# Layer 0's cross-attention: Pool's side jobs thinned out, queries loaded by pairs of groups, one transfer of shift rows a group

## The chip, the core and the metric

The kernel runs on one core of a Trainium2 chip. Its time is that of one execution on the device, in microseconds. The core has TensorE (PE: matmuls; PEld: its weight loads), VectorE (DVE), ScalarE (ACT), GpSimd (POOL) and SyncE (SP), which here only issues DMAs. Each engine has its own instruction stream, and they wait for each other by semaphores. TensorE's granted clock has two levels, 1.2 and 2.4 GHz.

## What is computed

Two transformer layers on x of 8 samples, 512 tokens and 320 features, with a context of 64 tokens and 192 features a sample. Each layer has self-attention, cross-attention to the context and a gated feed-forward, each behind a layer norm and with a residual. Layer 1 has also quantization to 8 bits in its attentions. The part in question, of layer 0:

```python
def _attn(x, ctx, wq, wk, wv, wo, bo, heads):       # heads = 20, dh = 16
    q = (x @ wq).reshape(b, n, heads, dh).transpose(0, 2, 1, 3)
    k = (ctx @ wk).reshape(b, j, heads, dh).transpose(0, 2, 1, 3)
    v = (ctx @ wv).reshape(b, j, heads, dh).transpose(0, 2, 1, 3)
    a = softmax(einsum('bhid,bhjd->bhij', q, k) * dh ** -0.5, axis=-1)
    return einsum('bhij,bhjd->bhid', a, v).transpose(0, 2, 1, 3).reshape(b, n, heads * dh) @ wo + bo
...
h2 = _ln(x, n2_g, n2_b)
x = _attn(h2, context, q2, k2, v2, o2_w, o2_b, heads) + x
h3 = _ln(x, n3_g, n3_b)
a, g = split(h3 @ ff_w1 + ff_b1, 2)
x = a * gelu(g) @ ff_w2 + ff_b2 + x
```

## The kernel before

`transformer` calls one function a phase, each with a block of its own that all engines enter and leave together. For layer 0: `dense_phase` (q, k, v), `self_attention`, `dense_phase` ("q": output projection of the self-attention, queries of the cross-attention), `cross_attention`, `dense_phase` ("ff"). Products in float32 precision are made of parts: each weight is held as `hi` and `lo` (`Split`), and each activation as well.

`cross_attention` (1892 to 2184) works in 40 groups of 4 heads of one sample (`NQ` = 40, `PER` = 5 groups a sample). In a group, two heads stand together in each of two halves `pr`. A group passes through these steps:

- SP loads the queries into `q_stack`, a ring of 8 groups (`RING`), three DMAs a group (hi, hi, lo; L1976), keys of a sample (six DMAs, L1966) and values (two, L1986).
- TensorE's `natural`: 8 matmuls of scores with the tokens on the partitions (`nat`, L2030). DVE takes the negated maximum of each row, `neg_max` (L2169).
- Pool splits `neg_max` into three bf16 parts with four instructions (`parts`, L2129 to L2132). The tile `parts` is single: Pool waits until TensorE has turned those of the group before.
- TensorE turns the parts into rows (`turn_shift`, L2047), ACT copies them to `shift_sb` (L2102) and issues two DMAs from it into rows 96 to 101 of `q_stack`, one a half (L2105).
- TensorE's `transposed`: the scores once more with keys on the partitions, the maximum taken off by those rows (`sT`, L2039). ACT makes the exponentials, `probs` (L2097).
- TensorE's `products` with the values (`o_ps`, L2057), ACT's copy `o_sb` (L2111), TensorE's `turn_output` (L2065), DVE's division and `o_nat`, SP's store to `cross_out` (L2013).

The order is written out by hand: all engines count n from -3 to 42, and TensorE does in round n `natural(n + 3)`, `transposed(n)`, `turn_shift(n + 2)`, `turn_output(n - 2)`, `products(n - 1)`. ACT does in round n the exponentials of n, the shift rows of n + 2 and the copy of `o_sb` for n - 1.

Pool has side work behind the `parts` of each group n. `PoolLoader.turn(pool, n)` (L274) starts the transfer of weight job n into one of two stage buffers and splits job n - 1 into `hi` and `lo` (L261 to L271); there are ten jobs, two for `wo2`, two for the first 256 rows of `ff_w2` and six for its other 1024 rows. `EarlyBias.add` (L306) adds the output bias to a 128-token tile of the residual x, 32 tiles in all, in groups 0 to 31.

`dense_phase` "ff" starts with the output projection of the first sample, statistics, `rstd` on Pool (L808), the norm, the transposes `zT` and then `ff1` and `ff2` products over ten chunks (`ff2` at L895). Where it is called with `next_weights`, as in layer 1, Pool runs all jobs of its loader directly behind the first `rstd`, before its bias add of the first sample (L824), and TensorE waits for them before the first chunk that is not in `ws[1]`.

Of the kernel before, what the change touches and what calls it, by code (L numbers as in the profile page):

```python
# [25 lines left out]
ALU = mybir.AluOpType  # L26
# [4 lines left out]
P = 128  # L31
# [3 lines left out]
FF = 1280  # L35
# [61 lines left out]
def words(t):  # L97

    return t.bitcast(F32)


def rows(ap, start, n):
    return ap[bass.ds(start, n), :]
# [1793 lines left out]
def cross_attention(nc, s, k, q, kk, v, out, next_weights, bias):  # L1897
# [3 lines left out]
    ROWS = QROWS + 6  # L1901
    N_Q, N_K, N_V = 3, 6, 2

    with ExitStack() as ctx:
# [21 lines left out]
        def exists(n):  # L1926
            return 0 <= n < NQ
# [12 lines left out]
        def shift_bank(n):  # L1940
# [6 lines left out]
            **{f"x_q_loaded{r}": 16 * N_Q * NQ // RING for r in range(RING)},  # L1947
            **{f"x_k_loaded{r}": 16 * N_K * len(range(r, BATCH, KEYS)) for r in range(KEYS)},
            **{f"x_v_loaded{r}": 16 * N_V * BATCH // 2 for r in range(2)},
            **{f"x_shift_loaded{r}": 32 * NQ // 2 for r in range(2)},  # L1950
# [19 lines left out]
        with nc.Block() as block:  # L1970

            @block.sync
            def _(sp):
                def load_q(n):
                    for quadrant, part in enumerate((0, 0, 1)):
                        sp.dma_start(words(q_stack[32 * quadrant:32 * quadrant + 32, n % RING]),  # L1976
                                     rows(q[part], n * 64, 64).rearrange("(x r) t -> r x t", r=32)
                                     ).then_inc(s[f"x_q_loaded{n % RING}"], 16)
# [13 lines left out]
                for n in range(1, LOOK):  # L1992
                    load_q(n)
                wait(sp, "x_cleared", 2)
                load_v(0)
                for n in range(LOOK, RING):
                    load_q(n)
# [3 lines left out]
                for n in range(FIRST, LAST):  # L2001
                    b = n // PER
                    if exists(n - 1) and exists(n - 1 + RING):
                        wait(sp, "x_turn_free", uses["scores", n - 1] + 1)
                        load_q(n - 1 + RING)
                    if exists(n - 1) and n % PER == 0 and b - 1 + KEYS < BATCH:
                        load_k(b - 1 + KEYS)
# [12 lines left out]
            def _(pe):  # L2020
                def natural(n):
                    wait(pe, f"x_q_loaded{n % RING}", 16 * N_Q * (n // RING + 1))
# [12 lines left out]
                def transposed(n):  # L2035
                    wait(pe, f"x_shift_loaded{n % 2}", 32 * (n // 2 + 1))
# [46 lines left out]
            def _(act):  # L2083
# [9 lines left out]
                for n in range(FIRST, LAST):  # L2093
# [5 lines left out]
                    if exists(n + 2):  # L2099
                        wait(act, "x_turn_full", uses["shift", n + 2] + 1)  # L2100
                        wait(act, f"x_shift_loaded{n % 2}", 32 * ((n + 2) // 2))
                        act.copy(shift_sb[:, n % 2, :], shift_bank(n + 2)).then_inc(s["x_turn_free"], 1)  # L2102
                        wait(act, "x_turn_free", uses["shift", n + 2] + 1)
                        for pr in range(2):
                            act.dma_start(words(q_stack[QROWS:ROWS, (n + 2) % RING, pr, :]),  # L2105
                                          words(shift_sb[6 * pr:6 * pr + 6, n % 2, :])
                                          ).then_inc(s[f"x_shift_loaded{n % 2}"], 16)
# [6 lines left out]
            def _(pool):  # L2114
# [9 lines left out]
                for n in range(NQ):  # L2124
                    wait(pool, "x_nat_free", 2 * (n + 1))
                    wait(pool, "x_turn_full", uses["shift", n - 1] + 1 if n else 0)
                    mine = neg_max[:, n % 4]
                    one, two, three = (parts[:, :, i:12:3] for i in range(3))
                    chained(pool.tensor_copy(one, mine), 3 * n + 1)  # L2129
                    chained(pool.tensor_tensor(rest[:, :, :], mine, one, ALU.subtract), 3 * n + 2)  # L2130
                    chained(pool.tensor_copy(two, rest[:, :, :]), 3 * n + 3)
                    pool.tensor_tensor(three, rest[:, :, :], two, ALU.subtract).then_inc(s["x_parts_ready"], 1)  # L2132
                    wait(pool, "x_parts_ready", n + 1)
                    loader.turn(pool, n)
                    if n < BATCH * TT:
                        early.add(pool, n)

            @block.vector
            def _(dve):
# [22 lines left out]
                for n in range(FIRST, LAST):  # L2162
                    if exists(n + LOOK):
                        m = n + LOOK
                        for pr in range(2):
# [3 lines left out]
                            dve.tensor_reduce(neg_max[:, m % 4, :, 2 * pr:2 * pr + 2],  # L2169
# [428 lines left out]
def transformer(nc, inputs, out):  # L2598

    with ExitStack() as ctx:  # L2600
# [43 lines left out]
        with ExitStack() as own:  # L2644
# [6 lines left out]
            w2 = [Split(nc, s, own, "ff_w2", rows(w["ff_w2"], 0, 2 * P), over=wo),  # L2651
                  Split(nc, s, own, "ff_w2", rows(w["ff_w2"], 2 * P, FF - 2 * P))]
            cross_attention(nc, s, k, q20, k20, v20, cross_out, [wo2, *w2], w["o2_b"])
            dense_phase(nc, s, k, 0, "ff", w["n3_g"], w["n3_b"], [w1, *w2], wo2, cross_out,
                        ff_bias=(w["ff_b1"], w["ff_b2"]))
# [40 lines left out]
```

## Time and profile before

| | |
|---|---|
| median of 3 runs | 3332.75 us (3332.37 to 3335.26) |
| profiled execution | 3331.84 us, its span 3330.1 us |
| TensorE matmul busy | 2940.8 us (88%) |
| VectorE | 2159.1 us (65%) |
| ScalarE | 1893.9 us (57%) |
| GpSimd | 808.3 us (24%) |
| layer 0's cross-attention in the span | about 850 to 1027 us |

Times in rows are from the span's start. Busy time of DMA-issuing instructions isn't counted. In a timeline a row gives start, duration, engine, line, operation, output tile, input tiles, count, and in brackets the idle time of the engine before it with what ended it. Durations of matmuls overlap: the distance from one start to the next is what they cost.

### The profile page before, as it was taken

To read this page: it belongs to the slowest core of one execution; us is meant where nothing else is said; L and a number is where in the kernel's file an instruction comes from. 1 tells how busy PE (TensorE), PEld (TensorE's weight loads), DVE (VectorE), ACT (ScalarE), POOL (GpSimd) and SP (SyncE) were. 2 spreads that over 40 slices of the span, in tenths; PEclk is the share of its full clock that TensorE was granted. 3 is DMA by queue.
4 is the path that set the end of the run, shared out by engine and by line. 5 is a ranking of instruction groups with operands and counts; after the bars stand their busy time and mean duration, and the time that the engine had idled before them with its cause. 6 is when DMAs were issued, how large, how long until landed. Compare 5 with 4: busy or idle time off the path is not lost. (4 is left out here: it accounts for less than half of the span.)

```text
span 3330.1 us, 47965 instructions
## 1 busy us (share of the span) xinstructions
PE 2940.8 (88%) x15582; PEld 1777.5 (53%) x15594; DVE 2159.1 (65%) x3834; ACT 1893.9 (57%) x3214; POOL 808.3 (24%) x1149
## 2 busy tenths in 40 slices
PE   6989999978796999998969999889979576899999
PEld 5754444457454888886841111111127332788888
DVE  5668888837353444444749999978868685444443
ACT  4338888845353232233549999999975355333322
POOL 2021222114640000000027878200003470200000
PEclk9979999989698999998975555555559888899999
DMA  8663333336662000001567566266722213010000
GB/s 229 211 167 101 108 106 103 90 81 162 162 177 47 10 10 19 9 0 32 152 174 167 125 143 138 58 91 91 96 49 97 80 45 92 26 36 18 25 17 16
DMA packets 358435, 296.57 MB, mean 89 GB/s; under 512 B 175794, under 2 KB 282106, under 8 KB 358250
## 3 DMA queue, kind: packets, MB, share of 16 engines
q1 hardware_dynamic: 348750, 274.52, 34.1%
q0 software_dynamic: 7280, 18.07, 2.1%
q8 instruction: 94, 1.54, 0.2%
q10 hardware_dynamic: 2220, 1.70, 0.2%
q14 instruction: 91, 0.75, 0.1%
HBM read 177.53 MB, written 114.52 MB: 88 GB/s over the span
## 5 line engine op out<-in xcount | busy, mean ns | idle before, releaser
L1599 PE MATMUL nat<-k_stack,q_stack 48*128 48x512 bf16 x640 | 383.6, 604 | 65.2 <-DMA k_stack<-k1w 23.6
L1395 DVE TENSOR_REDUCE neg_max<-nat 128x1 f32<-128x512 f32 x640 | 400.7, 682 | 59.7 <-PE nat L1254 59.6
L808 POOL TENSOR_TENSOR rstd<-var_eps,neghalf 128x4 f32<-128x4 f32 x48 | 51.9, 1082 | 1577.8 <-DVE var_eps L1032 1577.8
L1633 DVE TENSOR_REDUCE m_all<-nat 128x1 f32<-128x512 f32 x640 | 425.0, 691 | 13.8 <-PE nat L1599 13.5
L1653 ACT ACTIVATE nat<-nat,m_all 128x512 f32<-128x512 f32 x640 | 428.4, 2143 | 0.0
L1653 ACT ACTIVATION_READ_ACCUMULATOR nat<-nat,m_all 128x1 f32 x640 | 410.0, 1687 | 0.0
L1058 DVE SCALAR_TENSOR_TENSOR ff<-outp,bias,gel 128x512 f32<-128x512 f32 x160 | 120.1, 751 | 418.5 <-PE outp L326 418.5
L1329 ACT ACTIVATE probs<-sT 128x1024 f32<-128x1024 f32 x320 | 328.2, 1027 | 89.8 <-PE sT L1263 81.4
L972 ACT ACTIVATE gel<-outp,bias 128x512 f32<-128x512 f32 x160 | 110.2, 689 | 351.4 <-PE outp L326 351.4
L1852 ACT ACTIVATE exps<-sT 128x1024 f32<-128x1024 f32 x320 | 293.4, 1568 | 0.8 <-PE sT L1798 0.8
L976 ACT CAST ff_hi<-ff 128x512 fp32r<-128x512 f32 x160 | 99.2, 620 | 313.1 <-DVE ff L1058 313.1
L1599 PEld LDWEIGHTS nat<-k_stack,q_stack 48*128 48x128 bf16 x640 | 64.3, 101 | 384.0 <-ACT nat L1653 354.2
L1889 DVE TENSOR_SCALAR probs<-exps 128x1024 bf16<-128x1024 f32 x320 | 218.2, 692 | 59.7 <-ACT exps L1852 59.7
L1254 PE MATMUL nat<-k_stack,q_stack 48*128 48x512 f32 x640 | 199.9, 522 | 20.3 <-DMA k_stack<-k_hi 11.9
L1798 PE MATMUL sT<-q_stack,k_stack 51*128 51x512 bf16 x640 | 193.9, 603 | 26.8 <-DMA q_stack<-shift_rows 4.1
L1281 PE MATMUL o_ps<-probs,v_stack 128*32 128x256 f32 x2560 | 198.2, 391 | 1.1 <-issue 1.1
L1061 DVE TENSOR_TENSOR ff_lo<-ff,ff_hi 128x512 fp32r<-128x512 f32 x160 | 122.1, 763 | 109.8 <-ACT ff_hi L976 109.8
L1052 DVE TENSOR_TENSOR hT_lo<-h,hT_hi 128x512 fp32r<-128x512 f32 x144 | 111.8, 781 | 106.3 <-ACT hT_hi L967 106.0
L1254 PEld LDWEIGHTS nat<-k_stack,q_stack 48*128 48x128 f32 x640 | 79.8, 192 | 163.4 <-DVE neg_max L1395 131.7
L1263 PE MATMUL sT<-q_stack,k_stack 51*128 51x512 f32 x640 | 156.9, 428 | 0.5 <-ACT probs L1329 0.2
L326 PE MATMUL outp<-hT_hi,Wff_hi 128*128 128x512 f32 x320 | 125.8, 393 | 4.7 <-DVE hT_lo L1052 4.7
L326 PE MATMUL outp<-hT_hi,w_hi 128*128 128x512 f32 x320 | 126.0, 394 | 3.4 <-DVE hT_lo L1052 3.4
(561 smaller groups left out, 7075.4 us busy)
## 6 DMA issues: line engine op xcount, KB each, us to landing
v<-vpad SPq DMA_DIRECT2D x64, 320.0 KB, 2.8
q_stack<-q_part SPq DMA_DIRECT2D x90, 160.0 KB, 5.9
k_stack<-k1w SPq DMA_DIRECT2D x90, 160.0 KB, 10.6
q_stack<-q_hi SPq DMA_DIRECT2D x160, 64.0 KB, 2.6
v_stack<-v SPq DMA_DIRECT2D x40, 256.0 KB, 3.2
q_stack<-q_hi SPq DMA_DIRECT2D x80, 128.0 KB, 2.8
raw<-v SPq DMA_DIRECT2D x16, 640.0 KB, 11.9
k_stack<-k_hi SPq DMA_DIRECT2D x158, 64.0 KB, 2.2
```

The costliest lines, as they stand in the source:

```text
L326: mm = pe.matmul(out, stay, move, start=(n == 0), stop=(n == len(terms) - 1))
L1254: pe.matmul(nat[(16 * n + t) % 3][:, :], q_stack[half, n % RING, pr, qt * P:(qt + 1) * P], k_stack[half, n % RING, pr, :], start=True, sto ...
L1263: mm = pe.matmul(sT[use % 2][:, ab, :], k_stack[half, n % RING, pr, kt * P:(kt + 1) * P], q_stack[half, n % RING, pr, :], start=True, stop ...
L1281: mm = pe.matmul(o_ps[VCOL * h:VCOL * h + VCOL, tok], v_stack[:, n % 2, kt, VCOL * h:VCOL * h + VCOL], probs[:, n % 2, h, kt, tok], start= ...
L1329: act.activation(probs[:, n % 2, 2 * pr:2 * pr + 2, kt, :], sT[use % 2][:, :, :], ACT.Exp, scale=DH ** -0.5).then_inc(s["a_turn_free"], 1)
L1395: dve.tensor_reduce(neg_max[:, n % 2, qt, 2 * pr + ab:2 * pr + ab + 1], nat[(16 * (n + 2) + t) % 3][:, :], AX.X, ALU.max, negate=True).the ...
L1599: pe.matmul(bank[i % NAT][:, :], q_stack[half, slot, g, pr, qt * P:(qt + 1) * P], k_stack[half, slot, g, pr, :], start=True, stop=True).th ...
L1633: dve.tensor_reduce(k.m_all[:, column(i // TILES, i % TILES)], bank[i % NAT][:, :], AX.X, ALU.max, negate=True).then_inc(s["e_max_ready"], 1)
L1653: act.activation(b[:, :], b[:, :], ACT.Exp, bias=k.m_all[:, col], accum_out=k.s_all[:, col]).then_inc(s["a_nat_free"], 1)
L1798: mm = pe.matmul(sT[u % TURNS][:, ab, :], k_stack[half, slot, g, pr, kt * P:(kt + 1) * P], q_stack[half, slot, g, pr, :], start=True, stop ...
L1852: act.activation(exps[:, u % EXPS], sT[u % TURNS][:, :, :], ACT.Exp).then_inc(s["a_turn_free"], 1)
L1889: dve.tensor_scalar(probs[:, u % KEPT], exps[:, u % EXPS], ROUND, -ROUND, ALU.add, ALU.add).then_inc(s["e_rounded"], 1)
```

## The change

- `next_weights` of layer 0's cross-attention loses the last 1024 rows of `ff_w2` (six of ten Pool jobs); they go to the feed-forward phase behind it, which now is called with `next_weights`.
- The four jobs that stay have their turn behind groups 3, 7, 11, 15 and 19 instead of 0 to 10, and the bias adds go with groups 8 to 39 instead of 0 to 31.
- Queries come by pairs of groups: three DMAs a pair in place of six of half the size, a semaphore a pair; the reload of a ring slot waits for the later group of its pair.
- The shift rows of a group come with one DMA of twelve rows. For that the columns of `parts` alternate between the halves: `neg_max` is written with stride 2, and Pool's views of it are split in two.

```diff
@@ cross_attention
+    PAIRS = RING // 2
...
-            **{f"x_q_loaded{r}": 16 * N_Q * NQ // RING for r in range(RING)},
+            **{f"x_q_loaded{r}": 16 * N_Q * NQ // RING for r in range(PAIRS)},
...
-            **{f"x_shift_loaded{r}": 32 * NQ // 2 for r in range(2)},
+            **{f"x_shift_loaded{r}": 16 * NQ // 2 for r in range(2)},
...
-                def load_q(n):
+                def load_q(pair):
+                    r = pair % PAIRS
                     for quadrant, part in enumerate((0, 0, 1)):
-                        sp.dma_start(words(q_stack[32 * quadrant:32 * quadrant + 32, n % RING]),
-                                     rows(q[part], n * 64, 64).rearrange("(x r) t -> r x t", r=32)
-                                     ).then_inc(s[f"x_q_loaded{n % RING}"], 16)
+                        sp.dma_start(words(q_stack[32 * quadrant:32 * quadrant + 32, 2 * r:2 * r + 2]
+                                           ).rearrange("r u x t -> r (u x) t"),
+                                     rows(q[part], pair * 128, 128).rearrange("(y r) t -> r y t", r=32)
+                                     ).then_inc(s[f"x_q_loaded{r}"], 16)
...
                 load_q(0)
                 wait(sp, "x_first_cleared", 1)
                 load_k(0, (1,))
-                for n in range(1, LOOK):
-                    load_q(n)
+                load_q(1)
                 wait(sp, "x_cleared", 2)
                 load_v(0)
-                for n in range(LOOK, RING):
-                    load_q(n)
+                for pair in range(2, PAIRS):
+                    load_q(pair)
                 load_k(1)
                 load_v(1)
                 load_k(2)
                 for n in range(FIRST, LAST):
                     b = n // PER
-                    if exists(n - 1) and exists(n - 1 + RING):
+                    if exists(n - 1) and exists(n - 1 + RING) and n % 2 == 0:
                         wait(sp, "x_turn_free", uses["scores", n - 1] + 1)
-                        load_q(n - 1 + RING)
+                        load_q((n - 1 + RING) // 2)
                     if exists(n - 1) and n % PER == 0 and b - 1 + KEYS < BATCH:
+                        wait(sp, "x_turn_free", uses["scores", n - 1] + 1)
                         load_k(b - 1 + KEYS)
...
-                    wait(pe, f"x_q_loaded{n % RING}", 16 * N_Q * (n // RING + 1))
+                    wait(pe, f"x_q_loaded{n // 2 % PAIRS}", 16 * N_Q * (n // RING + 1))
...
-                    wait(pe, f"x_shift_loaded{n % 2}", 32 * (n // 2 + 1))
+                    wait(pe, f"x_shift_loaded{n % 2}", 16 * (n // 2 + 1))
...
-                        wait(act, f"x_shift_loaded{n % 2}", 32 * ((n + 2) // 2))
+                        wait(act, f"x_shift_loaded{n % 2}", 16 * ((n + 2) // 2))
                         act.copy(shift_sb[:, n % 2, :], shift_bank(n + 2)).then_inc(s["x_turn_free"], 1)
                         wait(act, "x_turn_free", uses["shift", n + 2] + 1)
-                        for pr in range(2):
-                            act.dma_start(words(q_stack[QROWS:ROWS, (n + 2) % RING, pr, :]),
-                                          words(shift_sb[6 * pr:6 * pr + 6, n % 2, :])
-                                          ).then_inc(s[f"x_shift_loaded{n % 2}"], 16)
+                        act.dma_start(words(q_stack[QROWS:ROWS, (n + 2) % RING, :, :]), words(shift_sb[0:12, n % 2, :])
+                                      ).then_inc(s[f"x_shift_loaded{n % 2}"], 16)
...
-                    mine = neg_max[:, n % 4]
-                    one, two, three = (parts[:, :, i:12:3] for i in range(3))
+                    mine, left = (x.rearrange("p t (a r) -> p t a r", a=2) for x in (neg_max[:, n % 4], rest[:, :, :]))
+                    columns = parts[:, :, 0:12].rearrange("p t (a i r) -> p t a i r", a=2, i=3)
+                    one, two, three = (columns[:, :, :, i, :] for i in range(3))
...
-                    loader.turn(pool, n)
-                    if n < BATCH * TT:
-                        early.add(pool, n)
+                    if n % 4 == 3 and n // 4 <= len(loader.jobs):
+                        loader.turn(pool, n // 4)
+                    if n >= NQ - BATCH * TT:
+                        early.add(pool, n - (NQ - BATCH * TT))
...
-                            dve.tensor_reduce(neg_max[:, m % 4, :, 2 * pr:2 * pr + 2],
+                            dve.tensor_reduce(neg_max[:, m % 4, :, pr:4:2],
@@ transformer
-            w2 = [Split(nc, s, own, "ff_w2", rows(w["ff_w2"], 0, 2 * P), over=wo),
-                  Split(nc, s, own, "ff_w2", rows(w["ff_w2"], 2 * P, FF - 2 * P))]
+            w2 = [Split(nc, s, own, "ff_w2", rows(w["ff_w2"], 0, 2 * P), over=wo)]
             cross_attention(nc, s, k, q20, k20, v20, cross_out, [wo2, *w2], w["o2_b"])
+            w2.append(Split(nc, s, own, "ff_w2", rows(w["ff_w2"], 2 * P, FF - 2 * P)))
             dense_phase(nc, s, k, 0, "ff", w["n3_g"], w["n3_b"], [w1, *w2], wo2, cross_out,
-                        ff_bias=(w["ff_b1"], w["ff_b2"]))
+                        ff_bias=(w["ff_b1"], w["ff_b2"]), next_weights=w2[1:])
```

## Rows read from the trace of the kernel before

**Rows 1.** The page, part 2: granted TensorE clock in 40 slices, in tenths.
```profile
PEclk9979999989698999998975555555559888899999
```

**Rows 2.** Timeline of PE in the cross-attention: start, duration, instruction, idle before.
```profile
856.04 3.90 PE L2030 MATMUL nat<-k_stack,q_stack 96*128 96x128 f32 x16 [10.46 <-DMA k_stack<-k_hi]
...
867.31 1.22 PE L2039 MATMUL sT<-q_stack,k_stack 102*128 102x512 f32 x2 [0.81 <-DMA q_stack<-shift_sb]
871.78 0.61 PE L2047 MATMUL sT<-identb,parts 128*32 128x128 bf16 x4 [3.25 <-POOL parts L2132]
...
877.22 0.61 PE L2047 MATMUL sT<-identb,parts 128*32 128x128 bf16 x4 [1.97 <-POOL parts L2132]
...
879.66 1.97 PE L2030 MATMUL nat<-k_stack,q_stack 96*128 96x128 f32 x8
...
886.01 1.97 PE L2030 MATMUL nat<-k_stack,q_stack 96*128 96x128 f32 x8
...
898.25 1.11 PE L2030 MATMUL nat<-k_stack,q_stack 96*128 96x128 f32 x8
...
901.73 1.11 PE L2030 MATMUL nat<-k_stack,q_stack 96*128 96x128 f32 x8
...
917.07 1.11 PE L2030 MATMUL nat<-k_stack,q_stack 96*128 96x128 f32 x8
```

**Rows 3.** Timeline of all engines there: ACT's DMA queue and Pool.
```profile
861.20 2.05 ACTq L2105 DMA_DIRECT2D q_stack<-shift_sb  x2
...
867.34 0.32 POOL L261 CAST tail_hi<-stage 128x160 fp32r<-128x160 f32 x1 [1.32 <-DMA stage<-in_L_xattn_o_w]
```

**Rows 4.** Windows: length, busy of five engines, granted clock, DMA share, GB/s.
```profile
851.00:858.00 7.00, 1.94 (x8) 1.81 (x9) 5.19 (x4) 2.18 (x2) 2.33 (x3) 0.50 0.88 219
...
197.90:245.80 47.90, 37.83 (x116) 18.70 (x116) 38.37 (x59) 13.58 (x15) 21.81 (x34) 0.50 0.53 133
849.90:897.80 47.90, 34.16 (x130) 22.19 (x130) 17.72 (x26) 12.73 (x17) 34.41 (x72) 0.50 0.73 169
...
877.20:897.70 20.50, 20.48 (x72) 11.34 (x74) 6.20 (x12) 6.77 (x10) 16.35 (x33) 0.50 0.44 123
...
221.90:245.70 23.80, 23.79 (x89) 12.16 (x88) 20.41 (x34) 12.91 (x14) 13.31 (x24) 0.50 0.41 119
...
1058.20:1065.00 6.80, 5.95 (x14) 4.70 (x15) 0.69 (x1) 2.04 (x3) 0.00 (x0) 0.50 0.01 2
```

**Rows 5.** Instructions on `q_stack`, 850 to 900 us: durations min/median/max in ns.
```profile
L1976 SPq DMA_DIRECT2D q_stack<-q_hi x26: 311/427/1132, 850.3 to 896.7; - x26
L2105 ACTq DMA_DIRECT2D q_stack<-shift_sb x14: 671/674/1328, 861.2 to 897.6; - x14
...
DMA to landing us min/median/max: 2.3/3.0/6.5
```

**Rows 6.** Timeline at the end of the phase: ACT and PE.
```profile
1008.71 0.59 ACT L2111 COPY o_sb<-o_ps 128x512 f32<-128x512 f32 x1 [1.51 <-issue]
...
1012.83 0.66 PE L2065 MATMUL o_ps<-ident,o_sb 128*128 128x128 f32 x4 [0.75 <-ACT o_sb L2111]
...
1016.29 0.66 PE L2065 MATMUL o_ps<-ident,o_sb 128*128 128x128 f32 x4 [1.13 <-ACT o_sb L2111]
```

**Rows 7.** Both feed-forwards' starts: one line of L895, timelines, a page group.
```profile
L895 PEld LDWEIGHTS yp<-ff_w_hi,ff_hi x256: 186/188/190, 1083.6 to 1547.1; 128*128 128x128 f32 x128
...
1059.05 0.79 PE L326 MATMUL outp<-hT_hi,w_hi 128*128 128x512 f32 x1 [3.42 <-DVE hT_lo L1052]
...
2845.01 0.80 PE L326 MATMUL outp<-hT_hi,Wff_hi 128*128 128x512 f32 x1 [4.71 <-DVE hT_lo L1052]
...
2850.94 0.87 POOL L271 TENSOR_TENSOR Wff_lo<-stage,Wff_hi 128x320 fp32r<-128x320 f32 x1
...
2852.87 2.40 DVE L1061 TENSOR_TENSOR ff_lo<-ff,ff_hi 128x512 fp32r<-128x512 f32 x1 [0.69 <-ACT ff_hi L976]
...
L1061 DVE TENSOR_TENSOR ff_lo<-ff,ff_hi 128x512 fp32r<-128x512 f32 x160 | 122.1, 763 | 109.8 <-ACT ff_hi L976 109.8
```

More of the change, by code:

```diff
@@ L2126, in _ @@
                     wait(pool, "x_turn_full", uses["shift", n - 1] + 1 if n else 0)
-                    mine = neg_max[:, n % 4]
-                    one, two, three = (parts[:, :, i:12:3] for i in range(3))
+                    mine, left = (x.rearrange("p t (a r) -> p t a r", a=2) for x in (neg_max[:, n % 4], rest[:, :, :]))
+                    columns = parts[:, :, 0:12].rearrange("p t (a i r) -> p t a i r", a=2, i=3)
+                    one, two, three = (columns[:, :, :, i, :] for i in range(3))
                     chained(pool.tensor_copy(one, mine), 3 * n + 1)
-                    chained(pool.tensor_tensor(rest[:, :, :], mine, one, ALU.subtract), 3 * n + 2)
-                    chained(pool.tensor_copy(two, rest[:, :, :]), 3 * n + 3)
-                    pool.tensor_tensor(three, rest[:, :, :], two, ALU.subtract).then_inc(s["x_parts_ready"], 1)
+                    chained(pool.tensor_tensor(left, mine, one, ALU.subtract), 3 * n + 2)
+                    chained(pool.tensor_copy(two, left), 3 * n + 3)
+                    pool.tensor_tensor(three, left, two, ALU.subtract).then_inc(s["x_parts_ready"], 1)
                     wait(pool, "x_parts_ready", n + 1)
-                    loader.turn(pool, n)
-                    if n < BATCH * TT:
-                        early.add(pool, n)
+                    if n % 4 == 3 and n // 4 <= len(loader.jobs):
+                        loader.turn(pool, n // 4)
+                    if n >= NQ - BATCH * TT:
+                        early.add(pool, n - (NQ - BATCH * TT))
             @block.vector
```

## The prediction, made blind

> **What bounds the kernel now.** The phases of the program stand one behind the other, so the question is what sets the length of one phase, layer 0's cross-attention (about 850 to 1027 us), and of the start of the feed-forward behind it, which takes over work. The page's clock row comes first [rows 1]: TensorE's granted clock has its lowest digit before 1700 us, a 6, in the eleventh slice (833 to 916 us), where this phase starts. Then the TensorE timeline of the phase [rows 2]. It has three regimes. Up to 877 us TensorE waits, above all on Pool's `parts` (3.25 us before 871.78, 1.97 before 877.22). Then it is dense at 1.2 GHz: one group takes 886.01 - 879.66 = 6.35 us. From 897.7 on it is dense at 2.4 GHz: 901.73 - 898.25 = 3.48 us a group. Both dense regimes are TensorE's own work: every kind of its matmuls shrinks at the change of clock, and no wait shows. One microsecond of dense work moved from the slow to the fast clock so gives back 1 - 3.48/6.35 = 0.45 us.
>
> Why Pool is late is in its own timeline: behind the `parts` of group 1 it issues the transfers of a weight job, waits 1.32 us for those of the job before [rows 3], splits the staged weight, adds a bias tile, and only then looks at group 2, whose shift transposes so start at 871.78 [rows 2].
>
> The windows [rows 4] show what TensorE did before its clock rose. Here: half from 849.9 to 897.8, dense for the last 20.5 us of it (20.48 busy). In layer 0's self-attention: half for the same 47.9 us, dense for the last 23.8. In the feed-forward, where the matmuls are 128 rows by 128 columns, the rise came some 6 us after the first of them (1059.05 [rows 7] to 1065).
>
> **The change, part by part.**
>
> *Pool in the first groups.* Gone from groups 0 to 10: ten weight jobs of some 3 us and eight bias adds of 0.86. The jobs that stay (four, for `wo2` and the first 256 rows of `ff_w2`) go after groups 3, 7, 11, 15 and 19. I walk the start with cold durations of the timeline (8 `nat` matmuls 1.8 us start to start, scores 1.1, shift transposes 0.5, output transposes 1.05, products 1.9). `nat` of group 0 was at 856.04 [rows 2]; I put it at 856.5 (the part on queries says why). Shift 0 860.4, `nat` 2 860.9, and Pool is free for `parts` 1, so shift 1 comes at 862.9 (863.99 before), `nat` 3 at 863.4. The first scores wait for the shift rows of group 0: copy done 861.7, one issue of 0.7, then the 4.1 us that passed before between the end of two issues (863.25 [rows 3]) and the scores (867.31): 866.5. Shift 2 follows at 867.6 (871.78 before), then `nat` 4 868.1, scores 1 869.9, shift 3 871.0, products 0 871.6, `nat` 5 873.5, and `nat` 6 at 879.9 where it was 886.01: 6.1 us ahead, at half clock still.
>
> *The clock.* TensorE is then dense from 866.5 instead of 877.2. If the rise comes as long after the dense stretch begins as it did in the two attention phases (20.5 and 23.8, mean 22.2), it is at 888.7. Group 7 starts at 886.25, has done 2.45 us at 6.36, and needs (1 - 0.385) x 3.48 = 2.14 more: `nat` 8 at 890.8, against 898.25 [rows 2]. **Lead 7.4 us.** With 20.5 us it is 8.3, with 23.8 us 6.7.
>
> *Later Pool stalls.* From 898.25 to 917.07 five groups took 18.8 us where five of 3.48 take 17.4 [rows 2]; the difference of 1.4 us is Pool's jobs again, and is gone. Jobs 1 and 2, after groups 7 and 11, take 4.1 to 4.4 us on Pool where a warm group leaves 2.4 before the next `parts` and 1.7 of slack behind it: I give back 0.4. **Net 1.0** (0 to 1.4).
>
> *Queries by pairs.* Half as many issues on SP's queue, the same bytes. Issues of q take 0.43 us [rows 5]; that one of double size takes as long is an assumption, and the phase's first keys come behind 768 KB instead of 384. From 851 to 858 the transfers ran at 219 GB/s [rows 4], and the first pair with the keys is 1.03 MB, 4.7 us of it: keys at 856 to 857.5 instead of 856.0, with what a landing takes. Cost 0.5 (0 to 1.5), already in the walk. Later a pair is asked for when the previous odd group's exponentials are done and is needed three groups on, 10.4 us at full clock; q took 3.0 us to land, 6.5 at most [rows 5], plus some 1.5 of issuing: hidden. If it were not, the excess would stand once in two groups. Keys of sample 1 now are needed at 873.5 rather than 879.7; the 4 MB up to and with them, at the same rate, end near 869 to 870. Hidden by some 3 us. The wait added before `load_k` is one that SP met before anyway (the q load stood in front); behind it are only loads of later samples.
>
> *One transfer of shift rows.* It removes one of two issues on ACT, 0.67 us each [rows 5]. In the warm groups ACT is back to back with them: copy of `o_sb` right behind the issues, 1.51 us after the instruction before [rows 6], and TensorE takes `o_sb` 0.1 us later. TensorE is as full, so there it buys nothing (0 to 0.06 a group). At the end of the phase, where there are no `nat` matmuls, TensorE waits 0.75 and 1.13 us for that copy [rows 6]: an issue less brings its 0.67 back at both. **1.3 us** (0.6 to 2). The rows show 0.67 us for 6 partitions and 0.43 for 32 rows of q twice as long, so an issue's price doesn't follow its bytes. The Trainium skill (DMA: Bandwidth & Descriptors, "Why a DMA increments its semaphore by 16 and not by 1") says why: a transfer is spread over the largest number up to 16 that divides the outer sizes of both sides, and the issuing sequencer itself writes the increments of the engines that are left out. By it the merged one (6 partitions by 2, from 12) has the old price once, as I take it.
>
> *Same arithmetic in another order.* Pool's four pieces and the reduction write as many elements through other strides: 0 (within 0.05 us a group, and Pool has slack).
>
> *Six weight jobs in the feed-forward.* Layer 1 already has this form, so its rows are the price [rows 7]. The jobs end at 2851.8, 6.8 us behind the first product of that phase (2845.01); layer 0 first needs `ff_w` 24.6 us behind its own (1083.6 against 1059.05): hidden by some 18 us. But the first product waited 4.71 us on `hT_lo` there and 3.42 here, since the subtractions on DVE run long beside Pool's; and the bias add, now behind the jobs, meets the first `ff_lo`, 2.40 us there against a mean of 0.76. I take 1.3 + 0.4 - 0.3 (part of it at the slow clock's end) = **1.4 us lost** (0.6 to 2.5). The Trainium skill (GPSIMD Engine Reference, "Specifications") names this: Pool shares its SBUF interface with VectorE when that one has two SBUF inputs. It speaks against this change, and the trace agrees by 2.40 against 0.76.
>
> **Sum**: 7.4 + 1.0 + 1.3 - 1.4 = 8.3 us. The profiled execution took 3331.84 (span 3330.1 and 1.7 around it), so 3323.5; the median of the runs, 3332.75, lies 0.9 above it: **3324.4 us**. Behind the phase the work stands otherwise against the clock's changes; I allow 1.5 us both ways.
>
> **Rivals.**
>
> *The clock rises by time since its fall.* For it: both attention phases had the half clock for the same 47.9 us [rows 4], though one was dense for 20.5 and the other for 23.8 us at the end. Against it: layer 1's self-attention stayed at half throughout, nine slices of the page in a row [rows 1]. The fall, before the phase, doesn't move, so the rise stays at 897.7. Then this kernel is at group 8.80 there, before at 7.84: lead 0.96 x 3.48 = 3.4. Sum 4.3, **3328.4 us**.
>
> *The clock rises some 6 us after TensorE gets dense*, as in the feed-forward [rows 4, 7]: at 872.5. That is 16.2 us earlier than above, 7.3 us more: **3317.1 us**. Against it: in this very phase 20.5 dense microseconds were needed. The Trainium skill (TensorE: Matmul & The Clock Gate, "What's actually happening") has sustained activity release the throttle, which would be this, and which this phase and the self-attention contradict.
>
> *Slower: the merged transfer's issue on ACT costs more than two did.* ACT has less than 0.1 us to spare in each of some 31 warm groups. From 1.46 us on each excess counts 31 times; the gain is gone at 1.46 + 8.3/31 = 1.73, and at 2.0 us the kernel takes 3324.4 + 31 x 0.54 = **3341 us**. For it: one issue took 1.33 [rows 5], and the new one walks two dimensions. Against it: the 0.43 of the larger q issues.
>
> *It doesn't do what it says*: the first scores and keys wait for transfers, so that Pool's removal only shows them. Then about half of the lead stays at the old rise: some 3 us, 3330.
>
> **Chances.** Forecast 0.55, by time since the fall 0.23, early rise 0.07, slower 0.08 (the issue, and what I don't see), not as it says 0.07. The forecast's own terms spread it over 3321 to 3328. The range is 3319 to 3331: it holds the forecast and both middle rivals, and leaves out the early rise and the slower case. A difference of 0.2% is 6.7 us, about what a measurement can tell from none: faster by more, 0.45 of the forecast's 0.55, the early rise, a little of the others: 0.54; within 0.38; slower 0.08.
>
> **What would show it.** In the changed kernel's TensorE timeline: no wait on `parts` before 877; first scores near 866.5, `nat` 6 near 880; dense from about 867. The clock's rise near 889 (the first rival: 897.7 again; the second: before 875). Groups of 3.48 behind it, with two short waits at most, near groups 8 and 12. ACT's issues one a group at 0.67, and waits on `o_sb` of about 0.1 and 0.5 at the end. Six jobs from about 1040 on, the first product's wait near 4.7 instead of 3.4. I am wrong if the keys of group 0 land after 857.5, if `nat` waits for q later on, or if the clock keeps its own time.

## The result, and the profile after

| | before | after |
|---|---|---|
| median, 18 runs each | 3332.21 us (3327.27 to 3338.94) | 3326.82 us (3320.41 to 3331.87) |
| ratio | | 0.9982, 95% interval 0.9976 to 0.9988 |
| profiled execution, its span | 3331.84, 3330.1 us | 3320.41, 3318.5 us |
| TensorE matmul busy | 2940.8 us | 2929.4 us |

The change is worth 5.4 us by the medians and 0.18% by the ratio. The interval excludes zero, but the gain is below the 0.2% that I had set apart: "faster by more", at 0.54, did not come, "within", at 0.38, did. The profiled execution of after is the shortest of its 18, so a comparison of the two traces flatters the change by some 6 us. All times of a trace count from its own span's start, and after's phase begins 3.2 us earlier, though no line ahead of it changed. So I measure from the first query issue of the phase (850.31 before; 847.11 after).

TensorE in the cross-attention of after (columns as in [rows 2]):

```profile
854.84 3.90 PE L2033 MATMUL nat<-k_stack,q_stack 96*128 96x128 f32 x16 [12.46 <-DMA k_stack<-k_hi]
...
868.73 1.22 PE L2042 MATMUL sT<-q_stack,k_stack 102*128 102x512 f32 x2 [5.10 <-DMA q_stack<-shift_sb]
...
870.43 1.97 PE L2033 MATMUL nat<-k_stack,q_stack 96*128 96x128 f32 x8
...
875.73 1.11 PE L2033 MATMUL nat<-k_stack,q_stack 96*128 96x128 f32 x8
...
886.17 1.11 PE L2033 MATMUL nat<-k_stack,q_stack 96*128 96x128 f32 x8
...
891.62 0.40 PE L2050 MATMUL sT<-identb,parts 128*32 128x128 bf16 x4 [0.34 <-POOL parts L2134]
...
905.87 0.40 PE L2050 MATMUL sT<-identb,parts 128*32 128x128 bf16 x4 [0.27 <-POOL parts L2134]
...
1002.45 0.66 PE L2068 MATMUL o_ps<-ident,o_sb 128*128 128x128 f32 x4 [0.50 <-ACT o_sb L2112]
...
1009.50 0.66 PE L2068 MATMUL o_ps<-ident,o_sb 128*128 128x128 f32 x4 [0.69 <-ACT o_sb L2112]
```

Pool is gone from the first groups: no wait on `parts` before 891.62, where before had 3.25 and 1.97 us. In its place stands 5.10 us in front of the first scores, for their shift rows. Behind 868.73 TensorE waits for nothing until 891 us, and the clock rises between 870.43 (`nat` of 1.97 us) and 875.73 (1.11 us). The windows (columns as in [rows 4]) say the same:

```profile
868.73:875.50 6.77, 6.77 (x24) 3.69 (x24) 1.39 (x2) 2.96 (x4) 3.46 (x11) 0.50 0.30 67
875.70:890.00 14.30, 14.30 (x93) 8.47 (x92) 7.88 (x16) 8.26 (x12) 6.14 (x20) 1.00 0.73 165
```

| us behind the first query issue | before | after | lead |
|---|---|---|---|
| first `nat` | 5.73 | 7.73 | -2.0 |
| first scores | 17.00 | 21.62 | -4.6 |
| `nat` of group 8 | 47.94 | 39.06 | 8.9 |
| last output transposes | 173.03 | 162.39 | 10.6 |
| first product of the feed-forward | 208.74 | 200.17 | 8.6 |
| end of the span | 2479.8 | 2471.4 | 8.4 |

### The profile page after: what moved, and what is told of

Same layout as the page of the kernel before. It is cut to its first block and busy times, and to the rows that moved or that the text cites. A ratio compares the mean times of both kernels' runs of the same rounds, so it can differ in the third digit from the quotient of the medians.

```text
span 3318.5 us, 47860 instructions
## 1 busy us (share of the span) xinstructions
PE 2929.4 (88%) x15582; PEld 1771.2 (53%) x15594; DVE 2162.3 (65%) x3834; ACT 1896.2 (57%) x3214; POOL 805.2 (24%) x1149
## 6 DMA issues: line engine op xcount, KB each, us to landing
k_stack<-k1w SPq DMA_DIRECT2D x90, 160.0 KB, 10.6
```

## Experiments

Each is timed against runs of the kernel before on the same chip, taken in between. Below, the dense start is the first matmul from which on TensorE waits for nothing until its clock rises, the rise is the moment at which its granted clock goes from 1.2 to 2.4 GHz, and +16.83 means 16.83 us behind the phase's first query issue.

### The change once more, and its three parts alone

The change again is the same code. The other three are the kernel before with one part of the diff shown above: the Pool part (turns, bias adds, the feed-forward's loader), the pair loads (`load_q`, its order and its waits), or the merged transfer (ACT's issue, its semaphores, and the columns that `parts` and `neg_max` need for it). Of each the line that matters, in this order:

```diff
-                    loader.turn(pool, n)
+                    if n % 4 == 3 and n // 4 <= len(loader.jobs):
+                        loader.turn(pool, n // 4)
```
```diff
-                def load_q(n):
+                def load_q(pair):
```
```diff
-                        for pr in range(2):
-                            act.dma_start(words(q_stack[QROWS:ROWS, (n + 2) % RING, pr, :]),
+                        act.dma_start(words(q_stack[QROWS:ROWS, (n + 2) % RING, :, :]), words(shift_sb[0:12, n % 2, :])
```

> The changed kernel once more, for a second trace of the same program. In the first trace the clock rose 6.8 us after TensorE became dense (868.73 to 875.5), where the prediction had 20.5 to 23.8. Theory A (the rise follows from what TensorE did before it, and that is the same in each execution): again 6 to 8 us after the first scores, and mean granted clocks of the timed runs that all lie at 0.844. Theory B (the moment of the rise is loose from one execution to the next): another moment in this trace, and runs spread over mean clocks 0.841 to 0.844, the shorter ones with the higher clock. Time 3326 to 3328 by both, 5 to 6 us below the kernel before.

3324.93 us against 3332.07, 7.1 below; ratio 0.9986 (0.9974 to 0.9997). The first scores came at +22.20. The rise came 6.5 us behind the dense start again, but theory A's other half fell: the runs spread from 3321.25 us at a mean clock of 0.844 to 3337.06 at 0.840.

> The kernel before with the Pool part of the change alone: four weight jobs behind groups 3, 7, 11, 15 and 19, bias adds from group 8 on, six jobs in the feed-forward; queries by single groups, two shift-row transfers. Theory A (Pool's removal carries the gain and the pair loads and the merged transfer cost time in the start): first scores about 17 us behind the phase's first query issue (21.6 in the changed kernel), no wait on parts before group 4, gain over the kernel before 8 to 12 us, more than the changed kernel's 5.4. Theory B (the parts need each other: with two issues and single loads the start waits for ACT or SP instead): gain 3 to 5 us. In both the feed-forward's first product comes 1.1 us later behind the end of the phase.

3322.38 us, 9.7 below; ratio 0.9974 (0.9964 to 0.9985). Theory A. In its trace the first query issue is at 849.86, so the first scores are at +16.83. The clause on the feed-forward missed: its first product comes 37.6 us behind the last output transposes, in the two traces of before 35.7 and 36.6, so it is 1.0 to 1.9 us later, where both theories had 1.1.

```profile
855.88 3.90 PE L2030 MATMUL nat<-k_stack,q_stack 96*128 96x128 f32 x16 [10.78 <-DMA k_stack<-k_hi]
...
866.69 1.22 PE L2039 MATMUL sT<-q_stack,k_stack 102*128 102x512 f32 x2 [1.61 <-DMA q_stack<-shift_sb]
...
894.91 0.40 PE L2047 MATMUL sT<-identb,parts 128*32 128x128 bf16 x4 [0.41 <-POOL parts L2132]
```

> The kernel before with the queries by pairs alone. Theory A (the first keys wait behind 768 KB): the first nat product about 2.0 us later behind the phase's first query issue (7.7 against 5.7), Pool and all behind it later by as much, 0.9 to 2 us slower, the rest unchanged. Theory B (hidden by Pool's work, which bounds the start anyway): within 0.3 us of the kernel before.

**3348.40 us, 16.3 above**; ratio 1.0053 (1.0040 to 1.0067). Both theories missed. The first `nat` did come 2.4 us late (8.11 behind the first query issue), but behind it stood what neither had, in the waits of TensorE from 885 to 1020 us (total, times, longest):

```profile
PE sT L2042 <- DMA q_stack<-shift_sb: 7.1, 10, 1.3
```

From the first query issue to the last output transposes the phase took 187.8 us, where before took 173.0. Of these 14.8 us the start has 6.3 (first scores at +23.28 for +17.00) and those waits 7.1.

> The kernel before with one transfer of shift rows a group alone (and the columns of parts in the other order). Theory A: the two waits for o_sb at the end of the phase (0.75 and 1.13 us) go, 1.3 to 1.9 us faster, nothing else, since Pool bounds the first groups. Theory B (the merged transfer lands later, 7.4 us behind its issue as in the changed kernel against 4.1): the first scores come 3 us later or more, of which Pool's 3.25 us wait behind them absorbs most; 0 to 1 us faster in all.

3330.78 us; ratio 0.9999 (0.9989 to 1.0009): unclear by the time. By its trace the tail is as theory A has it (the waits of 0.75 and 1.13 us are one of 0.50), and the first scores waited 0.28 us only, with 4.1 us from the end of the issue to the scores. So the merged form isn't what lands late.

### Taking one part away from the change

The kernel after, with the pair loads undone:

```diff
-                def load_q(pair):
+                def load_q(n):
```

with the merge undone:

```diff
-                        act.dma_start(words(q_stack[QROWS:ROWS, (n + 2) % RING, :, :]), words(shift_sb[0:12, n % 2, :])
+                        for pr in range(2):
+                            act.dma_start(words(q_stack[QROWS:ROWS, (n + 2) % RING, pr, :]),
```

with groups 0 and 1 loaded one by one (`load_one` issues the three DMAs of one group, as `load_q(n)` did):

```diff
-                load_q(0)
+                load_one(0, "x_q_first")
                 wait(sp, "x_first_cleared", 1)
                 load_k(0, (1,))
+                load_one(1, "x_q_loaded0")
                 load_q(1)
                 wait(sp, "x_cleared", 2)
```

and with the keys of sample 1 and the last pair behind the shift rows:

```diff
-                for pair in range(2, PAIRS):
-                    load_q(pair)
+                load_q(2)
+                wait(sp, "x_shift_loaded0", 16)
                 load_k(1)
+                load_q(3)
```

> The changed kernel with the queries loaded by single groups again (the Pool part and the merged shift transfer stay). Theory A (the pair loads cost what the changed kernel lacks against the Pool part alone, 3322.4 against 3324.9 to 3326.8: keys 2 us late, and shift rows 7.4 to 7.7 us from issue to scores instead of 3.6 to 4.1): first scores 15 to 17 us behind the phase's first query issue, no wait over 2 us behind the first nat, 3318 to 3322 us. Theory B (pairs are neutral, the difference was chance): 3325 to 3327, like the changed kernel. For the clock: if the single issue on ACT goes with the early rise (6 to 8 us after the dense work begins in the three traces with it, 18.7 to 20.7 in the three without), the rise comes again within 9 us; if that was chance, it may come after 18 to 21.

**3316.14 us, 14.8 below the kernel before**; ratio 0.9952 (0.9939 to 0.9964), apart from the change's own interval. Theory A, by 2 us more than its range. Some of it can be the clock: these five runs have means of 0.843 to 0.845, those of the kernel before 0.839 to 0.844. First query issue 848.43:

```profile
854.60 3.90 PE L2030 MATMUL nat<-k_stack,q_stack 96*128 96x128 f32 x16 [10.89 <-DMA k_stack<-k_hi]
864.78 1.22 PE L2039 MATMUL sT<-q_stack,k_stack 102*128 102x512 f32 x2 [1.38 <-DMA q_stack<-shift_sb]
```

The scores come at +16.35 instead of +21.62. The rise came 7.2 us behind the dense start.

> The changed kernel with two shift-row transfers a group again (the Pool part and the pair loads stay). Theory A (the second of the two transfers falls behind the double query load, as in the kernel with pairs alone, where ten of the later groups waited 0.3 to 1.3 us for their shift rows): again waits on the shift rows in every second group, 5 to 8 us of them, 3330 to 3336 us, so the merge is worth as much as that only beside the pairs. Theory B (those waits needed Pool's jobs beside them): no such waits, 3326 to 3328 us. For the clock: the rise 18 to 21 us after the dense work begins if it goes with the number of issues on ACT, otherwise 6 to 9.

3336.16 us, 5.2 above; ratio 1.0020 (1.0005 to 1.0035). Theory A for the waits: 6.1 us in ten, without most of Pool's jobs beside them. The rise came 12.5 us behind the dense start, between the two expectations for it. One such group, ACT's and SP's queues with TensorE's scores, in e9_no_merge:

```profile
919.74 1.55 SPq L1978 DMA_DIRECT2D q_stack<-q_hi  x2
920.20 1.39 ACTq L2108 DMA_DIRECT2D q_stack<-shift_sb  x2
921.34 0.43 SPq L1978 DMA_DIRECT2D q_stack<-q_lo  x1
...
925.37 0.73 PE L2042 MATMUL sT<-q_stack,k_stack 102*128 102x512 f32 x2 [0.28 <-DMA q_stack<-shift_sb]
```

and the same in after:

```profile
938.34 0.81 SPq L1978 DMA_DIRECT2D q_stack<-q_hi  x2
938.80 0.74 ACTq L2107 DMA_DIRECT2D q_stack<-shift_sb  x1
...
943.54 0.68 PE L2042 MATMUL sT<-q_stack,k_stack 102*128 102x512 f32 x2
```

A pair is issued in the very moment of the shift rows. Two issues end at 921.59; TensorE would use the rows 3.5 us later (925.37 - 0.28 - 921.59) and waits until 3.8. The single issue is over 0.65 us sooner (0.74 for 1.39) and leaves 4.0 us (943.54 - 939.54), and no wait shows.

> The changed kernel, but groups 0 and 1 come by single loads, group 0 ahead of the first keys and group 1 behind them. Theory A (the 2.0 us by which the first nat came late are the 384 KB more ahead of the keys): first nat 5.5 to 6.2 us behind the phase's first query issue instead of 7.7. The first scores move less, 0 to 1.5 us earlier, as the shift rows still wait for the loads issued before them; 0 to 1.5 us faster than the changed kernel. Theory B (the keys are late for their own issue or for the clearing of their tile): first nat stays at 7.7.

3324.74 us; ratio 0.9980 (0.9971 to 0.9989), the change's own. Theory A for the keys: first query issue 850.87, first `nat` 856.90, so +6.03. The first scores still waited 5.16 us, at +20.42.

> The changed kernel, but SP waits for the shift rows of group 0 before it loads the last pair of the ring, and the keys of sample 1 go ahead of that pair. Theory A (the shift rows land 7.4 us behind their issue because SP has issued all it may load by then, pairs at the price of single groups, and they pass behind those bytes): the first scores wait 1 to 2.5 us instead of 5.1, 17 to 19 us behind the first query issue instead of 21.6; later nat of groups 5 and 6 may wait up to 1 us for what was held back; 1.5 to 4 us faster than the changed kernel. Theory B (the landing is slow for another reason, such as the form of the merged transfer): the wait stays above 4 us and the held loads only come later.

3319.97 us; ratio 0.9964 (0.9954 to 0.9974). Theory A, and more than it asked: the wait is gone altogether. SP's and ACT's queues and TensorE:

```profile
861.37 0.43 SPq L1978 DMA_DIRECT2D q_stack<-q_lo  x1
869.45 0.94 SPq L1967 DMA_DIRECT2D k_stack<-k_hi  x2
...
866.36 1.40 ACTq L2108 DMA_DIRECT2D q_stack<-shift_sb  x1
...
868.09 1.97 PE L2034 MATMUL nat<-k_stack,q_stack 96*128 96x128 f32 x8
869.86 1.16 PE L2043 MATMUL sT<-q_stack,k_stack 102*128 102x512 f32 x2
```

SP goes on at 869.45, 1.7 us behind the end of ACT's issue (867.76): that is a landing with the last load issued 4.6 us ahead of ACT's issue (861.80 to 866.36), against 7.4 us in after. Scores at +16.46; nothing of what was held came late.

### Last four: combinations, and the clock

On top of `e8_no_pairs`, the shift rows first:

```diff
-                for n in range(LOOK, RING):
+                for n in range(LOOK, 6):
                     load_q(n)
+                wait(sp, "x_shift_loaded0", 16)
                 load_k(1)
+                for n in range(6, RING):
+                    load_q(n)
```

On top of that, in `dense_phase`, where Pool runs the jobs behind the first `rstd`:

```diff
                             for i in range(len(loader.jobs) + 1):
+                                if i == 1 and layer == 0:
+                                    name, count = bank_read(zT[2], b)
+                                    pool.wait_ge(s[name], count)
                                 loader.turn(pool, i)
```

On top of `e9_no_merge`, in SP's loop:

```diff
+                        wait(sp, f"x_shift_loaded{(n + 1) % 2}", 32 * ((n + 1) // 2 + 1))
                         load_q((n - 1 + RING) // 2)
```

> The kernel without pairs (Pool part and merged shift transfer; 3316.1 us), and SP waits for the shift rows of group 0 before it loads the keys of sample 1 and the queries of groups 6 and 7. Theory A (their landing is what the loads issued before them cost): the 1.38 us in front of the first scores go, first scores 15 us behind the first query issue instead of 16.35, 0.6 to 1.5 us faster: 3314.5 to 3315.5. Theory B: with single loads there is little ahead of the shift rows, and the wait stays: 3316.

3321.50 us (3316.36 to 3332.70); ratio 0.9970 (0.9955 to 0.9985). Neither theory's time. The first scores are at +15.70 with a wait of 0.40 us, so the edit did its 0.65 us. But its trace stayed at half clock for 24.9 us of dense work, the longest of all (windows, columns as above), and its runs follow their mean clock (3316.4 at 0.844, 3332.7 at 0.839). At a mean clock of 0.844 it takes what e8 takes there (3316.12), so no cost or gain of the edit shows.

```profile
866.23:890.90 24.67, 24.67 (x88) 14.39 (x90) 7.61 (x15) 9.15 (x13) 6.00 (x23) 0.50 0.62 148
```

> The kernel of e10_no_pairs_shift_first, and in layer 0's feed-forward Pool starts its first transfer but waits for the last hT_lo of the first sample before it splits a job. Theory A (the 1.0 us by which the first product came late are VectorE's subtractions beside Pool's, 1.22 and 1.39 us instead of 0.69): the subtractions take 0.69 to 0.9 again, the first product comes 8.1 to 8.3 us behind the first z transposes instead of 9.14, and the later jobs end some 16 us behind it, before the 24.6 us at which ff_w is needed; 0.8 to 1.1 us faster than e10. Theory B (the subtractions are long beside the transfers or for another reason): no difference.

**3316.20 us, 17.3 below**; ratio 0.9954 (0.9939 to 0.9968). Against e10 5.3 us less, of which the edit explains what its trace shows, 1.1 us. The rest goes with the clock: all six runs have means of 0.843 to 0.845, and e10's two at 0.844 took 3316.4 as well. Theory A for the start of the feed-forward, in e11:

```profile
1036.49 1.97 PE L855 MATMUL misc<-ident,z 128*128 128x128 f32 x8 [6.69 <-DVE z L1045]
...
1041.39 0.69 DVE L1055 TENSOR_TENSOR hT_lo<-h,hT_hi 128x512 fp32r<-128x512 f32 x1 [1.57 <-ACT hT_hi L970]
1043.66 0.69 DVE L1055 TENSOR_TENSOR hT_lo<-h,hT_hi 128x512 fp32r<-128x512 f32 x1 [1.57 <-ACT hT_hi L970]
1044.41 0.80 PE L326 MATMUL outp<-hT_hi,w_hi 128*128 128x512 f32 x1 [3.42 <-DVE hT_lo L1055]
```

and in after:

```profile
1038.14 1.97 PE L852 MATMUL misc<-ident,z 128*128 128x128 f32 x8 [6.77 <-DVE z L1042]
...
1043.04 1.22 DVE L1052 TENSOR_TENSOR hT_lo<-h,hT_hi 128x512 fp32r<-128x512 f32 x1 [1.58 <-ACT hT_hi L967]
1045.83 1.39 DVE L1052 TENSOR_TENSOR hT_lo<-h,hT_hi 128x512 fp32r<-128x512 f32 x1 [1.57 <-ACT hT_hi L967]
1047.28 0.79 PE L326 MATMUL outp<-hT_hi,w_hi 128*128 128x512 f32 x1 [4.64 <-DVE hT_lo L1052]
```

7.92 us from the transposes to the first product, against 9.14.

> The kernel without the merge (Pool part, pair loads, two shift transfers; 3336.2 us), and SP waits for the shift rows of group n + 1 before it loads a pair in round n. Theory A (the ten waits of 0.28 to 0.91 us are shift rows that pass behind the 768 KB of a pair issued in the same moment, with 4.2 us from issue to use where the round leaves 3.6): no wait on shift rows behind group 1, 5 to 8 us less: 3328 to 3331 us. Theory B (two small transfers of this form are slow by themselves beside any load): waits stay.

**3350.44 us**, 16.9 above, where theory A had 3328 to 3331; ratio 1.0069 (1.0044 to 1.0094). Waits of TensorE from 885 to 1020 us:

```profile
PE o_ps L2061 <- DVE o_nat L2152: 5.8, 4, 2.1
PE sT L2051 <- POOL parts L2136: 2.1, 2, 1.7
PE sT L2043 <- DMA q_stack<-shift_sb: 2.0, 3, 0.9
```

The shift rows' waits fell from 6.1 to 2.0 us, as theory A wants, and a new one of 5.8 us came. What is queued behind the waiting instruction on SP is the store of `o_nat`. DVE waits for a store, and TensorE for DVE:

```profile
906.66 0.26 DVE L2150 RECIPROCAL recip<-o_ps 128x16 f32<-128x16 f32 x1 [4.39 <-DMA cross_out<-o_nat]
...
907.43 1.08 PE L2061 MATMUL o_ps<-probs,v_stack 128*64 128x512 f32 x4 [1.45 <-DVE o_nat L2152]
```

The clock also fell twice in this phase.

> The kernel before once more, for a second trace. In its first one the clock rose 20.5 us after the dense work began; of the nine traces so far the rise came 6.5 to 8.2 us after it in four, 12.5 in one and 18.7 to 20.8 in the others, with no part of the change that sorts them. Theory A (the moment is set by the program's work): 20 to 21 us again. Theory B (it is loose): another distance, and a time on the shorter side of its runs if the distance is short.

3331.59 us; ratio 1.0003 (0.9992 to 1.0015). Theory B. (There were ten traces, five of them at 18.7 to 20.8, not nine.) The windows and TensorE's shift transposes in this second trace of the kernel before:

```profile
876.27:883.70 7.43, 7.43 (x28) 4.20 (x30) 1.78 (x4) 2.64 (x4) 6.49 (x12) 0.50 0.56 142
884.20:890.00 5.80, 5.63 (x38) 3.43 (x36) 3.19 (x6) 2.88 (x5) 4.79 (x11) 1.00 0.67 180
```
```profile
894.67 0.40 PE L2047 MATMUL sT<-identb,parts 128*32 128x128 bf16 x4 [1.32 <-POOL parts L2132]
...
899.53 0.40 PE L2047 MATMUL sT<-identb,parts 128*32 128x128 bf16 x4 [1.31 <-POOL parts L2132]
...
904.35 0.60 PE L2047 MATMUL sT<-identb,parts 128*32 128x128 bf16 x4 [1.27 <-POOL parts L2132]
```

The rise came 7.65 us behind the dense start, where it had been 20.5 in [rows 2, 4]. And it brought little: a group now takes 4.86 us (899.53 - 894.67), as long as Pool needs for its parts, its job and its bias tile. From the first `nat` to the last output transposes this execution took 166.87 us, the first one 167.30, though the clock was up 12 us sooner behind the first `nat`; a short fall around 905 us took some 3 of these back, and the first scores came 0.8 us later.

## Why the forecast held, and which of its steps did not

The time came out 2.4 us from the forecast and inside the range, and that was luck in good part: a start that came too late and a clock that rose too early came near to balancing, and so did the cost of the pairs and the worth of the merge. By two of my own signs of being wrong its account had failed: the keys of group 0 came at +7.73, which is 858.0 on the scale of before and past my 857.5, and the clock's rise was 10 us off.

**The start.** I had the first scores at 866.5, 16.2 us behind the first query issue; they came at +21.6. The step that failed is "Queries by pairs: cost 0.5 (0 to 1.5)", in two places. The keys behind 768 KB cost 2.0 us, beyond my bound, which e5 gives back (+6.03). And I took the landing of the shift rows (4.1 us) from the trace of before, though the change alters what stands in front of them: a pair's issue costs SP the same 0.43 us as a single's, so by the time ACT issues the shift rows, SP has put more bytes ahead of them. In before that was the queries of five groups and a part of the sixth (2 MB and some):

```profile
860.00 0.43 SPq L1976 DMA_DIRECT2D q_stack<-q_lo  x1
860.79 0.78 SPq L1976 DMA_DIRECT2D q_stack<-q_hi  x2
```

and in after those of all eight (3.1 MB), with the keys of sample 1 behind them:

```profile
857.03 0.50 SPq L1978 DMA_DIRECT2D q_stack<-q_lo  x1
857.57 0.94 SPq L1967 DMA_DIRECT2D k_stack<-k_hi  x2
...
859.94 1.40 ACTq L2107 DMA_DIRECT2D q_stack<-shift_sb  x1
```

From the end of ACT's issue to the scores it took 3.6 to 4.9 us with singles (before, its second trace e12, e1, e3, e8), 7.3 to 8.1 with pairs (after, e0, e2, e5, e9, e13), and with singles partly held back 3.0 and 3.2 (e11, e10); with the later pair held back the rows had landed after 1.7 (e6). The old issue price had been a brake. A third miss is small: the phase's first issue on ACT took 1.40 us where I wrote 0.7, though [rows 5] has 1.33 as its longest. The 5.4 us are 1.4 until the end of ACT's copy (the keys), 0.7 of that issue and 3.3 of landing. Undoing the pairs (e8) is worth more than the whole change, 0.9952 against 0.9982.

**Pairs in the warm groups.** "Hidden" holds only because of the merge. I asked whether the pair itself arrives in time, and not what it passes in front of.

**The merge.** I gave it 1.3 us, all in the tail. The tail is right: 0.75 and 1.13 us of waits became one of 0.50. Its real worth beside the pairs is some 9 to 12 us (e9 3336.2 against 3324.9 and 3326.8; +5.2 against -7.1 and -5.4 by the kernel before beside each), the ten waits of 6.1 us and 0.8 to 1.4 us at the first scores (+23.01) among it. In the warm groups I called an issue less worth 0 to 0.06 us because ACT's copy is the next thing late; the shift rows, too, had no time to spare there, and only before's single loads hid it. One issue took 0.74 us, a little more than the "old price once" of 0.67 and not 1.46 or more: the slower rival is out by its own condition.

**Pool and the clock.** My lead of 7.4 us came from 20.5 to 23.8 us of dense half clock before each rise. That was no rule: in the granted clock of 14 traces the rise of this phase came 6.5 to 24.9 us behind the dense start (six of them under 8.3), 20.5 and 7.65 for the same program. The rival by time since the fall is out as well: the half clock lasted 23.9 to 54.6 us. The early rise, to which I gave 0.07, is what the profiled execution of after did (6.8 us), and its 3317.1 us did not come because the start was late. Also the last rival, first scores and keys that wait for transfers, came true in part: 5.10 us of wait, beside the lead and not in its place. What sorts the cases I don't know. Two issues or one on ACT looked like it after six traces; e5 (one issue, 18.7 us) ended that.

The Pool term by itself I had at 7.4 + 1.0 - 1.4, with 0.5 of start cost taken in; e1 gives 9.7 (5 to 12 by its interval). The mechanism was right and one thing missing, which e12 shows: before, Pool was a second bound at 4.86 us a group up to group 10, so most of an early rise was lost on it. Thinned, the kernel keeps it. "Net 1.0" for later stalls is then only the price for a late rise; with an early one three stalls of 1.3 us stand there. Of the two short waits that I expected of the jobs that stay, near groups 8 and 12, both came: 0.34 and 0.27 us, 0.6 for my 0.4.

**Feed-forward.** Forecast 1.4 lost. From the `z` transposes to the first product it is 9.14 against 8.14 us, with two of three `hT_lo` at 1.22 and 1.39 us instead of 0.69 (and the first at 0.69 instead of 0.92), and e11, where Pool splits nothing before the last `hT_lo`, confirms Pool's work as the cause. The `ff_lo` that I added 0.4 for took 2.07 us, beside Pool's bias add, and no cost of it shows: from the first product to the span's end before has 2271.1 us and after 2271.2. A further 1.0 us of the table's 10.6 to 8.6 lies in the output projection, at half clock 2 us longer in after; the second trace of before has it too (28.5 us from the last output transposes to those of `z`, where the first has 27.6 and after 28.6), so it is chance.

**Sum.** In the profiled pair the phase and what follows gained 8.4 us where I had 8.3, by other terms. At `nat` of group 8 the lead was 8.9 us, forecast 7.4. The rise came 10 us earlier than forecast, worth 4.5 at 0.45 each; the start was 5.4 us late, and half-clock work that much later costs 5.4 x 0.55 = 3.0; 7.4 + 4.5 - 3.0 is the 8.9. With the rise where I had put it the lead would have been some 4.4, by this estimate. Over the rest of the phase 1.7 us were added (forecast 1.0 + 1.3), and in front of the first product 2.0 were lost (forecast 1.4). Over the runs the change is worth 5.4 and 7.1 us by the medians. Two small slips of the prediction change nothing: with 20.5 us its lead is 8.2, not 8.3, and 0.96 x 3.48 is 3.3, not 3.4.

## What to carry to other kernels

Ask of a transfer made larger or cheaper to issue not only whether it arrives in time, but which small, urgent transfer is issued next and now stands behind its bytes; hold the bulk until that one has landed. Before moving such a wait into a queue, list what else that queue carries: held in front of stores it cost more than it saved. And where a clock's change falls differently from run to run, price an edit at both moments, and take parts apart by runs: three parts worth -9.7, +16.3 and -1.3 alone made -5 to -7 together, and -14.8 without the middle one.

## Not expected of the hardware

- Shift rows of one group (24 KB, in one transfer) landed 1.7 us behind the end of their issue where no load had been issued for 4.6 us (e6). Behind the queries and keys that another engine had just issued by pairs, rows of the same size took 7.3 to 8.1 us to the scores that wait for them.
- An issue that walks twelve rows costs 0.74 us where six rows cost 0.67 each; the first one of the phase takes 1.3 to 1.4 in both forms, and as long while SP issues nothing (e6).
- The moment at which TensorE's clock rises in the same program, with the same dense work before it, differed by 13 us between two executions, and single short falls to half appeared in six of the 14 traces (e1, e2, e3, e9, e12, e13). Run times follow the mean granted clock: 3326 to 3329 us at 0.844 and 3331 to 3341 at 0.839 or 0.840 for the kernel before.
- On VectorE a subtraction of 0.69 us took 1.22 and 1.39 us while Pool subtracted, and 2.07 beside Pool's bias add (3.39 in e8 and e10).
